# A windowed-attention and ternary-FFN layer on one core: causal masks of all score groups through spare contraction rows, b2 added by GpSimd, queries placed by one doubled transfer per head

## The reference

```python
x = hidden                                    # (4, 2048, 256) float32
h = layernorm(x)
q, k, v = h @ Wq.T, h @ Wk.T, h @ Wv.T        # 16 heads of 16
s = q @ k.T / 4 + bias                        # -inf unless j <= i and j > i - 64
x = x + (softmax(s) @ v) @ Wo.T
h = layernorm(x)
W1, W2 = quantize(W1), quantize(W2)           # to -1, 0, 1 by the mean magnitude
x = x + relu(h @ W1.T + b1) @ W2.T + b2       # 256 -> 1024 -> 256
```

## Time and profile before

| | |
|---|---|
| median of 3 runs | 691.57 us (691.31 to 692.96) |
| the profiled execution | 696.39 us, span 694.6 us |
| mean granted TensorE clock | 0.980 of full speed |
| TensorE matmul busy | 653.9 us (94%) |
| VectorE busy | 611.0 us (88%) |
| ScalarE busy | 567.7 us (82%) |
| GpSimd busy | 556.4 us (80%) |
| SyncE's queue of transfers | 281848 packets, 42.43 MB |

### The profile page before, as it was taken

How to read it: one execution, slowest core, us unless ns; L and a number is a source line. 1 busy time by engine, 2 the same in 40 slices (tenths; PEclk the granted TensorE clock), 3 DMA queues, 4 the chain that set the end, 5 groups by cost and what they waited for, 6 DMA issues and landing times.

```text
span 694.6 us, 23901 instructions
## 1 busy us (share of the span) xinstructions
PE 653.9 (94%) x8048; PEld 557.4 (80%) x8048; DVE 611.0 (88%) x1391; ACT 567.7 (82%) x2489; POOL 556.4 (80%) x823
## 2 busy tenths in 40 slices
PE   7668789999999999999999999999999999998888
PEld 5446578888888888888878898888888888887776
DVE  4879889898999989899998999899899989897854
ACT  5588788898998988898988988898898988796622
POOL 7367899888888979888887989888898978887831
PEclk9889899999999999999999999999999999999999
DMA  8555563746465654736465564746465463643110
GB/s 291 77 104 114 90 111 62 142 81 114 78 130 96 132 98 92 134 78 118 85 132 96 115 117 90 123 82 122 85 131 98 90 114 58 122 81 78 32 39 31
DMA packets 314433, 70.59 MB, mean 102 GB/s; under 512 B 283076, under 2 KB 305862, under 8 KB 314312
## 3 DMA queue, kind: packets, MB, share of 16 engines
q1 hardware_dynamic: 281848, 42.43, 38.7%
q10 hardware_dynamic: 32464, 26.63, 13.2%
HBM read 20.25 MB, written 9.44 MB: 43 GB/s over the span
## 4 chain that ended last, share of the span: by engine, by line
PE 69%; SPq 7%; POOL 6%; DVE 6%; DMA 5%; ACT 4%; issue 3%; ACTq 0%; POOLq 0%; DVEq 0%
PE ps L1101 14%; PE ps L1089 11%; PE ps L1000 10%; PE ps L980 9%; PE ps L1037 8%; PE ps L1062 6%; PE ps L1048 4%; SPq L284 4%; DMA k<-kst 3%; SPq L304 3%; POOL tl L419 2%; PE ps L973 2%; PE ps L1074 2%; ACT p L523 2%; PE ps L1026 2%
## 5 line engine op out<-in xcount | busy, mean ns | idle before, releaser
L523 ACT ACTIVATE p<-ps,negm 128x96 f32<-128x96 f32 x1024 | 335.0, 355 | 16.9 <-DVE negm L724 16.3
L419 POOL TENSOR_TENSOR tl<-pt,th 128x384 f16<-128x384 f32 x256 | 234.4, 916 | 20.7
L523 ACT ACTIVATION_READ_ACCUMULATOR p<-ps,negm 128x1 f32 x1024 | 228.1, 223 | 0.0
L724 DVE TENSOR_REDUCE negm<-ps 128x4 f32<-128x384 f32 x256 | 138.2, 540 | 39.3 <-PE ps L980 36.3
L417 POOL CAST th<-pt 128x384 f16<-128x384 f32 x256 | 128.8, 503 | 32.0 <-DVE pt L741 31.8
L741 DVE STREAM_TRANSPOSE pt<-p 128x384 f32<-128x384 f32 x256 | 143.5, 561 | 3.0 <-ACT p L523 2.9
L980 PE MATMUL ps<-k,qbd 128*128 128x96 f16 x1536 | 125.6, 207 | 0.0
L980 PEld LDWEIGHTS ps<-k,qbd 128*128 128x128 f16 x1536 | 106.1, 99 | 11.1 <-issue 0.3
L1000 PE MATMUL ps<-th,vb 128*128 128x96 f16 (+1 forms) x1120 | 100.5, 205 | 2.2 <-DVE osum L800 1.6
L1000 PE MATMUL ps<-tl,vb 128*128 128x96 f16 (+1 forms) x1120 | 100.5, 205 | 0.0
L1000 PEld LDWEIGHTS ps<-th,vb 128*128 128x128 f16 x1120 | 96.4, 115 | 2.8 <-issue 1.7
(11 more groups left out here) (141 smaller groups left out, 1430.7 us busy)
## 6 DMA issues: line engine op xcount, KB each, us to landing
k<-kst SPq DMA_DIRECT2D x32, 288.0 KB, 4.0
vb<-vd SPq DMA_DIRECT2D x256, 32.0 KB, 2.0
rwide<-parked ACTq DMA_DIRECT2D x32, 256.0 KB
out<-x ACTq DMA_DIRECT2D x32, 256.0 KB, 3.7
qbd<-qs SPq DMA_DIRECT2D x254, 32.0 KB, 2.8
x<-in_L_attn_hidden ACTq DMA_DIRECT2D x15, 512.0 KB, 4.5
kw<-kst SPq DMA_DIRECT2D x31, 192.0 KB, 4.4
k<-kst SPq DMA_DIRECT2D x31, 144.0 KB, 3.8
```

Source lines behind the costliest of these rows:

```text
L419: e.tensor_tensor(tl[g % 2][:, o], pt[n % 3][:, :], th[g % 2][:, o], ALU.subtract).then_inc(s_lo, 1)
L523: ins = e.activation(p[:, 96 * u:96 * u + 96], bank[:, 96 * u:96 * u + 96], ACT.Exp, bias=m[:, u:u + 1], accum_out=r[:, u:u + 1])
L724: e.tensor_reduce(negm[n % 4][:, :], sbank[n % 3][:, 0:384].rearrange("p (a b) -> p a b", b=96), AX.X, ALU.max, negate=True).then_inc(s_mx, 1)
```

## The change

All four groups now use the second pass with the mask code: `qb[t]` holds both copies of the queries side by side (block, copy, 128), `kw` exists for four groups, and the mask matmul of line 973 is gone. ScalarE writes the high part twice (`qhi`, a broadcast read), and one transfer per head row moves both copies (64 KB); the low part has its own tile `qlo`. `place_q` has 8 transfers for either t, `place_k` 4 for either t. b2 is broadcast to 128 partitions once and GpSimd adds it to x after the normalisation (`add_b2`); the matmul of line 1096 is gone and the last residual waits for `s_b2`. At the start there are four `kw` mask copies instead of two, and two mask copies of queries instead of one. Slots are moved.

```diff
-V_LATE = 10
-A_T, A_Q, A_K, A_V = (1, 2), (5, 14), (6, 15), (10, 13)
-A_STATS, A_RSTD, A_NORM = (-24, -14), -12, (-7, -6)
-N_STATS, N_RSTD, N_NORM = ((-14, 1, 11), (-13, 2, 17)), (-12, 3, 21), ((-5, 7, 23), (-3, 9, 22))
-Q_DMA, K_DMA, V_DMA, A_CARRY = (7, 20), (15, 22), 17, 1
+V_LATE = 9
+A_T, A_Q, A_K, A_V = (1, 2), (6, 14), (6, 15), (10, 13)
+A_STATS, A_RSTD, A_NORM = (-25, -14), -11, (-7, -6)
+N_STATS, N_RSTD, N_NORM = ((-16, 1, 11), (-13, 2, 17)), (-11, 0, 21), ((-5, 7, 22), (-3, 11, 21))
+Q_DMA, K_DMA, V_DMA, A_CARRY = (7, 20), (15, 22), (18, 18), 2
+C_B2 = (13, 18)
-OUT_DMA, X_DMA = (23, 29), 36
-X_LATE = (8, 17, 25)
-PV_LAG, O_ADD, O_SPLIT = 8, 9, 15
+OUT_DMA, X_DMA = (23, 30), 36
+X_LATE = (6, 14, 23)
+PV_LAG, O_ADD, O_SPLIT = 8, 9, 14
-V_CLEAR = (15, 18, 22, 26)
-W_ABS = (1, 2, 3, 4)
+V_CLEAR = (19, 20, 24, 28)
+W_ABS = (0, 1, 2, 3)
...
 def place_k(e, c, t, groups=(0, 1)):
...
-                if t:
-                    e.dma_start(ks[g][:, :, :].rearrange("p m n -> p (m n)"),
-                                bass.AP(tensor=src, offset=row, ap=[[2 * w, 64], [0, 2], [1, 2 * w]])).then_inc(d_k[g], 16)
...
+                e.dma_start(ks[g][:, :], bass.AP(tensor=src, offset=row, ap=[[2 * w, 64], [0, 2], [1, w]])
+                            ).then_inc(d_k[g], 16)
+                e.dma_start(bass.AP(tensor=kw[g][:, :, :].tensor, offset=0, ap=[[2 * 1536, 64], [1, 1536]]),
+                            bass.AP(tensor=src, offset=row + w, ap=[[2 * w, 64], [32, 16], [1, 96]])).then_inc(d_k[g], 16)
...
+        def place_q(e, c, t, heads=((0, 1, 2, 3), (0, 1, 2, 3))):
...
+                    if v == 0:
+                        e.dma_start(bass.AP(tensor=to, offset=start, ap=[[2 * 8192, 16], [128, 64], [1, 32]]),
+                                    qhi[t][32 * h:32 * h + 32].rearrange("p b a j -> p (b a j)")
+                                    ).then_inc(d_q[t], 16)
+                    else:
+                        e.dma_start(bass.AP(tensor=to, offset=start, ap=[[2 * 8192, 16], [256, 32], [1, 32]]),
+                                    qlo[t][32 * h:32 * h + 32].rearrange("p b j -> p (b j)")).then_inc(d_q[t], 16)
...
+            def add_b2(h):
+                c, u = divmod(h, 2)
+                e.wait_ge(s_xnC, h + 1)
...
+                x2 = xs[c % NX][:, 2 * u:2 * u + 2, :]
+                e.tensor_tensor(x2, x2, b2w[:, :, :].to_broadcast([128, 2, D]), ALU.add).then_inc(s_b2, 1)
...
-                e.activation(qst[t][:, 0, :], a_bank(c, w)[:, :], ACT.Copy, scale=1 / WS).then_inc(s_ahi, 1)
+                e.activation(qhi[t][:, :, :, :],
+                             a_bank(c, w)[:, :].rearrange("p (b j) -> p b j", j=32).unsqueeze(2).to_broadcast([128, 16, 2, 32]), ACT.Copy, scale=1 / WS).then_inc(s_ahi, 1)
...
-                elif g >= 2:
-                    e.matmul(ends, identb[:, :], seen.unsqueeze(1).to_broadcast([128, 4, 2, 32]), start=True, stop=False,
-                             skip_group_check=True)
...
-                e.matmul(bank[:, o], ones[:, 0:128], bp[:, F:], start=True, stop=False)
```

More of the change, by code:

```diff
@@ L276, in place_q @@
                 e.wait_ge(s_zq, 1)
[L277 to L281, removed]
+                e.wait_ge(s_zm, t + 1)
+            for v, hs in enumerate(heads):
                 e.wait_ge((s_ahi, s_alo)[v], 8 * c + 3 + 4 * t)
                 for h in hs:
[L284 to L289, removed]
+                    to, start = qb[t][:, :, :, :, :].tensor, (32 * h + v) * 8192 + 32 * h
+                    if v == 0:
[5 more added lines that the diff above has]
+                                    qlo[t][32 * h:32 * h + 32].rearrange("p b j -> p (b j)")).then_inc(d_q[t], 16)
+        NQD, NKD = 8, 2
         block = ctx.enter_context(nc.Block())
@@ L329, in _ @@
                         place_k(e, c, t, (0, 1) if c or t else (1,))
[L330 to L333, removed]
+                for u in range(2):
+                    c = spread(n, V_DMA[u], 17)
+                    if c is not None:
+                        for m in range(2 * u, 2 * u + 2):
+                            place_v(c, m)
         @block.gpsimd
@@ L348, in mask_queries @@
                 e.wait_ge(d_s, 16)
-                e.tensor_copy(qm[:, :, :].rearrange("p g j -> p (g j)").bitcast(f32).rearrange("p (b j) -> p b j", j=64),
-                              pr[0][:, 0:64].unsqueeze(1).to_broadcast([128, 32, 64])).then_inc(s_zm, 1)
+                for t in range(2):
+                    e.tensor_copy(qb[t][:, :, :, 1, :].rearrange("p g b j -> p (g b) j").bitcast(f32),
+                                  pr[0][:, 0:64].unsqueeze(1).to_broadcast([128, 32, 64])).then_inc(s_zm, 1)
             def carry(c):
@@ L365, in biases @@
             def biases():
[L366 to L368 removed]
+                e.wait_ge(d_b, 32)
+                e.tensor_copy(bp[:, :], bt[:, :]).then_inc(s_bh, 1)
             def rstd_a(c):
@@ L450, in _ @@
                     low(n - L_PART)
+                for u in range(2):
+                    c = stage_c(n, C_B2[u])
+                    if c is not None:
+                        add_b2(2 * c + u)
                 ct = pair_at(n, R_MUL)
@@ L481, in mask_keys @@
                 e.wait_ge(d_km, 16)
-                for g in range(2):
+                for g in range(4):
                     e.activation(kw[g][:, :, :], kmask.unsqueeze(1).to_broadcast([128, 16, 96]), ACT.Copy).then_inc(s_kw, 1)
@@ L977, in scores @@
                     for m in range(2):
[L978 to L981, removed]
+                        keys = kw[g][:, blk, :] if m else ks[g][:, 32 * blk:32 * blk + 96]
+                        ins = e.matmul(bank[:, 96 * u:96 * u + 96], qb[g // 2][:, g % 2, blk, m, :], keys,
+                                       start=(not first and m == 0 and u == 0),
                                        stop=(m == 1 and u == 3), skip_group_check=True)
@@ L1101, in c_y @@
                         ins = e.matmul(bank[:, o], hT[hp][:, f, t * 128:(t + 1) * 128], w2T[:, f, :],
-                                       start=False, stop=(f == 7 and hp == 1))
+                                       start=(f == 0 and hp == 0), stop=(f == 7 and hp == 1))
                 if t:
```

62 lines of the change are left out of this document (29 added, 33 removed).

## The result

The changed kernel takes 714.16 us (708.91 to 720.85, 4 runs) beside 692.27 us before (691.31 to 693.03): ratio 1.0292, 95% interval 1.0206 to 1.0378. It is slower. The forecast was 691.0 and no change; the range ended at 701. The profiled execution took 710.62 us (span 708.8, clock 0.969), 14.2 us over the one of before, where the medians lie 21.9 us apart: the profiled execution of before is the longest of its kernel (696.39 us), that of the changed kernel one of the shorter ones.

A forecast was written before the change was run, and what follows sets the result against it. Two chains were taken as critical together, TensorE's period (39.18 us) and a loop through SyncE's queue (39.21). Loop -1, b2 at the end +0.5, start +0.9, before the loop -1: -0.6 from 691.6, so 691.0 us, range 676 to 701.

The forecast's parts named there:

- the loop: Values written, 24 issues on SyncE's queue, keys landed, TensorE's slots 8 to 13, values written again: 39.21 us a period before.
- the sum of the loop: Forecast period from values to values: 39.21 - 0.3 - 0.98 + 0.4 + 0.8 = 39.13 us, -1 us over 13 periods.
- The slack of 0.3 us: Before slot 8, keys were taken to land some 0.3 us early in periods in which TensorE didn't wait for them.
- The loop, TensorE's piece: Slot 8 to the score tile of slot 14: 7 mask and 2 b2 matmuls go, -0.98 us a period.
- The loop, the issues: SyncE's queue: 4 of 8 t = 1 query transfers carry twice the runs, +0.4 us a period (0 to 1.5).
- Values to keys: Stretch on SyncE's queue, forecast 18.2 to 18.7 us; under 18 points to full gain, over 19.3 to a backed-up queue.
- The loop, the keys: Group 2 needs two key transfers instead of one, keys ready later by 0.5 to 1.3 us a period, taken as 0.8.
- start and end together: Outside the loop: start net +0.9 us, b2 addition near the end +0.5, TensorE before the first loop period about -1.
- the queue backs up: Rival, chance 0.17: t = 1 queries on SyncE's full queue, +1.5 us a period, 711 us (701 with half the excess).

The follow-up runs named there:

- the run with b2 alone: Kernel before with only b2 moved to GpSimd (line 1096 out, `add_b2` in, positions 13 and 18): 693.10 us, ratio 1.0011.
- single queries: Changed kernel with the high part of the t = 1 queries sent to the first copy only (32 KB transfers instead of 64 KB): 696.99 us, ratio 1.0075.
- no low keys: Changed kernel without the transfer of the keys' low part for groups 2 and 3: 689.13 us, ratio 0.9936.
- the x load elsewhere: Changed kernel with the x load issued in slot 1 instead of slot 4 (X_DMA 33 for 36): 698.36 us, ratio 1.0096.

## Why the prediction was wrong

Right: the loop and where it shows, the order on the queue, the additions at 1.27 us (1269 ns), ScalarE's double write at 1.04 us (1024 ns), and that GpSimd and ScalarE stay hidden. That the 20 us taken from TensorE bring nothing was right as well.

The step that failed is the sum of the loop, 39.13 us; it measured 40.10, and 13 times the 0.97 between them is 12.6 us. (The loop grew by 0.89 a period, 11.5 of the 14.2 us between the two profiled executions.) Its terms, forecast and measured:

- **The slack of 0.3 us.** It was put at 0.3 without a row that shows it, and it wasn't there: in twelve of the thirteen periods of the kernel before TensorE began slot 8 within 0.15 us of the keys' landing. The five waits of the earlier trace rows are only a part of them.
- **The loop, TensorE's piece.** I took off 0.98 us for nine matmuls. Landing to values went from 17.17 to 16.48 us at the full clock, 0.69 less. The two matmuls of b2 are in this in full (0.21 in the run with b2 alone); the seven of the masks gave 0.48, since from the scores of slot 10 on the chain lies on VectorE and GpSimd (rows above), whose work didn't shrink.
- **The clock, which the sum doesn't have.** In three periods it fell to 0.50 after TensorE's pause before slot 8, for 3.4, 6.8 and 3.4 us: 5.4 us in all, 0.4 a period. The forecast had the clock at its upper level throughout.
- **The loop, the issues.** I took 0.4 us for the doubled query transfers, near the low end of 0 to 1.5. Values to keys rose by 0.6 on the mean and by up to 2.8 in single periods, those with an x load, of which there are ten and not nine.
- **The loop, the keys.** Taken as 0.8, measured 0.6 from first issue to the landing that slot 8 needs. This term was right.

In the profiled execution, then, most of the miss is a gain that didn't come (0.6 us a period of slack and masks) and the clock (0.4); the queue itself lost 1.2 us on queries and keys together, as much as forecast. It is the queue all the same from which the time comes back: single queries, no low keys and the x load elsewhere give 17, 25 and 16 us of device time. The median lies 3.5 us above the profiled execution; what its other executions do more, no trace shows.

**Outside the loop.** I forecast +0.4 us for start and end together; it was 2.7. The first values came 0.65 us later (103.39 for 102.74), and from the last values to the end it took 84.1 us instead of 82.1.

**The signs.** TensorE's busy time in the thirteen periods was to fall by 16 us and fell by 4 (502.10 to 497.92, in windows of 509 and 521 us); it holds the matmuls that ran at the lower clock. Idle time of 1.8 us a period at slot 8 for a transfer of keys came as said. Values to keys, at a mean of 18.8 us, lies between "right" (up to 18.7) and "the queue backs up" (over 19.3), and three single periods are over 19.3.

The rival that I gave 0.17, the backed-up queue, said 701 to 711 us and a decision at 1.3 us a period. It came nearest: the place and the x load are those that it named, and the runs that relieve the queue there bring the time back. By its own condition it was met in four of the thirteen periods only; on the mean queries and keys lost 1.2 us. That was enough because the gain against it was 0.7 and not 1.3. The time, 714, lies above even its 711. My chances had counted the two pieces as alternatives within the forecast's range, where both fall on the same chain.

The changed kernel's runs spread over 12 us, before over 2. A queue with varying stalls would spread them so; no run shows that it is the reason.

## What to carry to other kernels

When a chain through a queue is as long as the busiest engine's own work (here 39.2 us a period, with TensorE busy 38.6), work taken from the engine gives little and work added to the queue counts in full. A busy share of 98.6% doesn't say which of the two is the bound. The starts do: if in each period the first matmul follows the landing by the same 0.14 us, the queue is the bound and has no slack to spend. Transfers added where the DMA engines' share is already 1 should be priced at their full engine time; moving another load away from them (one constant, 16 us) was worth more here than reordering them (8 us). And before moving a product on TensorE to an earlier slot, ask what wait it was filling.

## What the runs showed of the hardware

Beside other traffic on the DMA engines the issuing instruction itself grows: the same query transfer of 64 KB holds SyncE's queue for 0.67 us (median) and up to 2.9 us, the longest beside the load of x.

What the added traffic cost the engines can be estimated from the rows of SyncE's queue on the profile pages, before and after (packets, MB, share of 16 engines' span):

```profile
q1 hardware_dynamic: 281848, 42.43, 38.7%
```
```profile
q1 hardware_dynamic: 347012, 46.23, 43.8%
```

The share of the span is 268.8 us of all 16 engines before and 310.5 after. So 65,164 packets more, most of them runs of 64 and 192 bytes, took 41.6 us, an estimated 2.6 us a chunk: 11 us for each added MB, where the queue's mean before was 6.3.

The Trainium skill (DMA: Bandwidth & Descriptors, section Why small descriptors are slow (HBM only)) exempts SBUF to SBUF transfers from the cost of short runs. The added traffic is of that kind, so the estimate speaks against it, as far as the fuller engines don't account for the difference. The landings of the changed kernel alone don't decide it, since the keys' low part, in runs of 192 bytes, is the larger transfer:

```profile
kw<-kst SPq DMA_DIRECT2D x63, 192.0 KB, 4.0
k<-kst SPq DMA_DIRECT2D x63, 144.0 KB, 3.5
qb<-qhi SPq DMA_DIRECT2D x128, 64.0 KB, 3.4
```

Leaving that part out was worth 25 us, but this is the price of the whole transfer; no run changes the run length alone.

The granted clock fell from 1.00 to 0.50 in three periods after TensorE had stood still for 2.0, 3.9 and 2.5 us before slot 8. In the last of them it fell only 0.7 us after TensorE had begun to work again, and was back 4 us after that beginning. A pause of that length doesn't always bring it: with b2 back on TensorE pauses of 2.6 and 3.1 us passed at the full clock.
